# A selective scan with steps spread over GpSimd and ScalarE, and a softmax filter run as a three-tile pipeline

## The chip, the cores and the metric

The kernel is one program on one core of a Trainium2 chip. The metric is device time in microseconds (us) from launch to end; lower is better. The median of three runs of the kernel before is 19240.01 us (19239.32 to 19246.41).

## What is computed

The input is a float32 image batch of 4 x 64 channels x 64 x 64. Four layers follow one another; the change touches parts of three of them.

- Layer 0: convolutions, normalisation, and then a selective scan (Mamba) over all 4 x 4096 tokens with 128 inner channels and 16 states. Each image starts from a state of zero.
- Layer 1: two selective scans over rows and over columns, with 192 inner channels and 96 states. Nothing of it is changed.
- Layer 2: a filter. A 3x3 convolution to 32 channels, a leaky ReLU and a 1x1 convolution give nine logits for each pixel; their softmax gives nine weights.
- Layer 3: a second selective scan of 16 states over one sequence of 16384 tokens, then projection, layer norm, SiLU and a residual.

The core of the two scans and of the filter:

```python
def step(h, t):                       # 16 states, 128 channels
    d, b, c, xt = t                   # d: softplus step, xt: silu of a 4-tap convolution
    h = h * jnp.exp(d[:, None] * A) + (d * xt)[:, None] * b[None, :]
    return (h, h @ c)
y = (ys + xc * D) * jax.nn.silu(z)    # out projection (and in layer 3: layer norm, silu, + x)

w_lp = softmax(conv1x1(leaky(conv3x3(x))))         # layer 2: nine weights a pixel
w_hp = delta_center - w_lp
high = sum over the 9 shifts k of shifted(x, k) * w_hp[k]
return x + high
```

## The kernel before, in words

A sequence of stages shares the core; each is a block with its own instruction streams, joined by semaphores, and streams are hand-ordered. In time: `phase_conv_norm` (to 274 us), `phase_mamba` for layer 0 (to 1616 us; here **m0**), two `phase_axis` stages (to 17242 us), `phase_filter` (to 17757 us), `phase_mamba` for layer 3 (to the end; here **m3**, the one with `final`). The names in the profile have lost their stage digits: `m_` is both m0 and m3.

**The scan stages.** Tokens go in 32 tiles of 512. For each tile `i` and state `n` of 16, the engines do this:

- TensorE (PE): `pb` (L662) spreads B's row n over 128 partitions into one of three PSUM banks, `pc` (L664) spreads C's row n, and `add` (L650) sums an earlier `gv` into `py`. `pb` waits until the scan three states back has freed its bank.
- ScalarE (ACT): `av` (L570) is exp(dt * A), `cv` (L573) copies `pc` out of PSUM. `pc` n waits for `cv` n-1.
- VectorE (DVE): the product `pb * dx` (L462), and one state behind it the scan (L468), which writes `hs`.
- GpSimd (POOL): `gv = hs * cv` (L604). Nothing else.

Between these, at a fixed state n, each engine has steps of the tile ahead (i+1) and the tile behind (i-1). For the tile ahead PE runs `in_proj` (L625; two matmuls, waits for the tile's input `u`), `gate_proj`, `x_proj`, `dt_proj`. ACT runs two tanh, `high`, `softplus`, then `middle` (L539), a logarithm (L543) and, in m3, the logarithm and exponential of `rsqrt` (L552, L554). DVE runs `silu` (L410, L412), `gates`, `remainder` (L420), `low` and `steps` (dt L428, dx L430). For the tile behind DVE runs `gated`, and in m0 `out_plain`, in m3 `norm` and `out_silu` (L453, L457). Two matmul forms occur throughout: bf16 ones, and float32 ones, which the trace shows as two records each.

After state 15 DVE copies the last column of all 16 states to `st` times `keep` (L501), and waits for it; every scan of the next tile starts from `st`. A product of tile i+1 also waits for dx.

SyncE (SP) issues all DMAs in one order: for each i it waits for `gate_proj` of i, loads `u` for i+2 (L338, L339), waits until the output tile `ot` of i is done (`s_done`), stores it (L345) and loads the residual for i+2 (L342). So the input for tile i+3 is issued only after output i is done:

```python
sync.wait_ge(s_xz, i + 1)
load_input(i + 2, p)
sync.wait_ge(s_done, i + 1)
store(i)
load_residual(i + 2, p)
```

In m3 the output of i is done by `out_silu(i)`, the last thing that DVE does in tile i+1; PE's `in_proj(i+3)` stands at n = 4 of tile i+2.

**The filter stage.** 16 tiles of two half-batches, one after another, in one chain: nine 3x3 taps (L1602, float32 matmuls), bias on ACT, leaky ReLU on DVE (L1543), logits, softmax in small DVE steps (L1545 to L1557) with one Exp on ACT, transpose by PE (L1618), copy on ACT, then for each of nine weights a float32 matmul with `sel` (L1626, two PSUM banks) that spreads it over the channels, a DVE product with the shifted image (L1566) and a DVE add (L1574), last `2 x - total` (L1577), and six stores. The taps of tile i+1 stand between the logits and the transpose of tile i.

Of the kernel before, what the change touches and what calls it, by code (L numbers as in the profile page):

```python
# [12 lines left out]
F32 = mybir.dt.float32  # L13
# [8 lines left out]
TOK = 512  # L22
# [202 lines left out]
def phase_mamba(nc, sem, ident_in, tag, w, u_s, res_s, out_s, reset, final):  # L225
# [6 lines left out]
    with ExitStack() as ctx:  # L232
# [79 lines left out]
        s_sq, s_var, s_rs, s_pn, s_tn = (sem(tag + n) for n in ("squares", "var", "rstd", "normed", "silu_tanh"))  # L312
# [10 lines left out]
        with nc.Block() as block:  # L323
# [40 lines left out]
            def _(dve):  # L364
# [12 lines left out]
                if reset:  # L377
                    v.memset(keep[:].rearrange("p (b t) -> p b t", t=TPB)[:, :, TPB - 1], 0.0)
# [47 lines left out]
                def steps(T, tp):  # L426
                    dve.wait_ge(s_sp, T + 1)
                    v.tensor_tensor(dt[:, tp], dt[:, tp], sp[:], ALU.add).then_inc(s_dt, 1)  # L428
                    dve.wait_ge(s_dt, T + 1)
                    v.tensor_tensor(dx[:, tp], dt[:, tp], xc[:], ALU.mult).then_inc(s_dx, 1)  # L430

# [4 lines left out]
                def residual_ready(T, tp):  # L436
                    dve.wait_ge(s_res[tp], T * 8 + (16 if tp == 0 else 8))

                def out_plain(T, tp):
                    dve.wait_ge(s_o, T + 1)  # L440
                    dve.wait_ge(s_out, 16 * T + 16)
                    residual_ready(T, tp)
                    v.tensor_tensor(ot[:], py[0:C, tp], res[:, tp], ALU.add).then_inc(s_done, 1)

                def norm(T):
                    dve.wait_ge(s_rs, T + 1)
                    v.tensor_tensor(n3[:], n1[:], n2[:], ALU.mult).then_inc(s_pn, 1)
                    dve.wait_ge(s_pn, 3 * T + 1)
                    v.tensor_scalar(n1[:], n3[:], half[:, 1:2], half[:, 2:3], ALU.mult, ALU.add).then_inc(s_pn, 1)

                def out_silu(T, tp):
                    dve.wait_ge(s_tn, T + 1)
                    v.scalar_tensor_tensor(n3[:], n2[:], 1.0, n1[:], ALU.add, ALU.mult).then_inc(s_pn, 1)  # L453
                    dve.wait_ge(s_pn, 3 * T + 3)
                    dve.wait_ge(s_out, 16 * T + 16)
                    residual_ready(T, tp)
                    v.tensor_tensor(ot[:], n3[:], res[:, tp], ALU.add).then_inc(s_done, 1)  # L457
# [6 lines left out]
                def scan(i, n):  # L464
                    un = i * NS + n
# [1274 lines left out]
```

## Time and profile before

| what | us |
|---|---|
| median of three runs | 19240.01 |
| the profiled execution | 19243.72 |
| span of its instructions | 19241.8 |
| m0, filter, m3 (by window) | 1342, 515, 1485 |
| busy: PE, DVE, ACT, POOL | 16257.4, 17802.0, 13962.1, 15292.2 |

Busy time is a mean over stages with other limits; the two axis stages take 15626 us of the span. A timeline row gives the start, the duration and, in brackets, the idle time of that engine before it and what ended it; the duration of a DVE instruction is longer than the distance to the next one's start, as they overlap by about 0.1 us. A matmul row with x2 is one float32 matmul.

### The profile page before, as it was taken

What the parts mean: (1) busy time and instruction counts of PE and PEld (TensorE: products, weight loads), DVE (VectorE), ACT (ScalarE), POOL (GpSimd) and SP (SyncE); (2) the same over time, 40 slices, a digit from 0 to 9 for tenths busy, and PEclk for the clock granted to TensorE, in tenths of its full rate; (3) what the DMA queues carried; (4) which work ended last, traced back from release to release, by engine and by line L of the source; (5) the groups of instructions that cost most, each with busy time, mean ns of one, the idle gap of its engine ahead of it and who ended that gap; (6) DMA issues with size and microseconds to landing.
All of it is one profiled execution on the core that took longest, in us unless ns stands there. A gap on an engine that the chain in (4) does not pass through costs nothing. (4 is left out here: it accounts for less than half of the span.)

```text
span 19241.8 us, 290646 instructions
## 1 busy us (share of the span) xinstructions
PE 16257.4 (84%) x60328; PEld 8303.8 (43%) x60424; DVE 17802.0 (93%) x48666; ACT 13962.1 (73%) x18390; POOL 15292.2 (79%) x10500
## 2 busy tenths in 40 slices
PE   5776888888888888888688888888888888887777
PEld 2223444444444444444344444444444444442222
DVE  4998999999999999999899999999999999984888
ACT  4665777777777777777577777777777777761666
POOL 1554999889888998888699999999999999970444
PEclk8998999999999999999899999999999999996999
DMA  1000000000000000000000000000000000000000
GB/s 33 13 13 12 11 11 11 11 11 11 11 11 11 11 11 11 11 11 11 12 11 11 11 11 11 11 11 11 11 11 11 11 11 11 11 10 20 10 12 11
DMA packets 778173, 227.53 MB, mean 12 GB/s; under 512 B 747760, under 2 KB 750476, under 8 KB 776332
## 3 DMA queue, kind: packets, MB, share of 16 engines
q1 hardware_dynamic: 776332, 206.79, 8.2%
q8 instruction: 691, 11.32, 0.3%
q14 instruction: 1150, 9.42, 0.2%
HBM read 143.66 MB, written 62.97 MB: 11 GB/s over the span
## 5 line engine op out<-in xcount | busy, mean ns | idle before, releaser
L1222 POOL TENSOR_TENSOR h_sm<-h_sm,h_wr 128x768 f32<-128x768 f32 x2944 | 5400.3, 1834 | 755.2 <-DVE h_wr L1002 669.6
L1222 POOL TENSOR_TENSOR w_sm<-w_sm,w_wr 128x768 f32<-128x768 f32 x2944 | 5399.1, 1834 | 502.5 <-DVE w_wr L1002 404.6
L1386 PE MATMUL w_pz<-w_xr,w_tri 128*128 128x384 f32 x9984 | 4462.6, 530 | 788.2 <-DVE w_wr L1002 622.5
L1386 PE MATMUL h_pz<-h_xr,h_tri 128*128 128x384 f32 x9984 | 4424.7, 526 | 770.6 <-DVE h_wr L1002 604.5
L1002 DVE SCALAR_TENSOR_TENSOR h_wr<-h_pz,h_bct,h_rbuf 128x192 f32<-128x192 f32 x11776 | 4250.3, 407 | 171.9 <-PE h_pz L1386 171.2
L1002 DVE SCALAR_TENSOR_TENSOR w_wr<-w_pz,w_bct,w_rbuf 128x192 f32<-128x192 f32 x11776 | 4243.4, 408 | 96.1 <-PE w_pz L1386 95.5
L976 DVE SCALAR_TENSOR_TENSOR w_xr<-w_cbuf,w_bct,w_pdx 128x192 f32<-128x192 f32 x9984 | 3634.9, 405 | 76.0 <-issue 35.2
L976 DVE SCALAR_TENSOR_TENSOR h_xr<-h_cbuf,h_bct,h_pdx 128x192 f32<-128x192 f32 x9984 | 3632.6, 404 | 75.7 <-issue 35.2
L1098 ACT ACTIVATE h_cbuf<-h_pe_e,h_consts 128x1024 f32<-128x1024 f32 x2304 | 2526.1, 1112 | 1532.4 <-PE h_pe_e L1374 1332.1
L1098 ACT ACTIVATE w_cbuf<-w_pe_e,w_consts 128x1024 f32<-128x1024 f32 x2304 | 2526.1, 1112 | 1492.7 <-PE w_pe_e L1374 1305.1
L604 POOL TENSOR_TENSOR m_gv<-m_hs,m_cv 128x512 f32<-128x512 f32 x1024 | 1351.0, 1322 | 2240.9 <-DVE m_hs L468 2213.4
L1121 ACT ACTIVATE w_rbuf<-w_pe_e,w_consts 128x1024 f32<-128x1024 f32 x2304 | 2476.3, 1113 | 0.0
L1121 ACT ACTIVATE h_rbuf<-h_pe_e,h_consts 128x1024 f32<-128x1024 f32 x2304 | 2476.2, 1113 | 0.0
L1386 PEld LDWEIGHTS w_pz<-w_xr,w_tri 128*128 128x128 f32 x9984 | 1516.5, 191 | 2027.4 <-DVE w_wr L1002 1647.7
L1386 PEld LDWEIGHTS h_pz<-h_xr,h_tri 128*128 128x128 f32 x9984 | 1516.5, 191 | 1974.5 <-DVE h_wr L1002 1604.6
L1374 PE MATMUL h_pe_e<-h_decay,h_lt 128*128 128x256 bf16 x9216 | 1782.1, 275 | 105.3 <-ACT h_rbuf L1121 88.8
L1374 PE MATMUL w_pe_e<-w_decay,w_lt 128*128 128x256 bf16 x9216 | 1773.2, 274 | 105.6 <-ACT w_rbuf L1121 88.7
L1374 PEld LDWEIGHTS h_pe_e<-h_decay,h_lt 128*128 128x128 bf16 x9216 | 915.3, 101 | 1337.2 <-issue 679.2
L1374 PEld LDWEIGHTS w_pe_e<-w_decay,w_lt 128*128 128x128 bf16 x9216 | 895.6, 99 | 1277.9 <-issue 709.0
L468 DVE TENSOR_TENSOR_SCAN m_hs<-m_av,m_st,m_pb 128x512 f32<-128x512 f32 x1024 | 1292.5, 1267 | 55.7 <-ACT m_av L570 54.7
L1231 POOL TENSOR_TENSOR w_cbuf<-w_cbuf,w_dxs 128x384 f32<-128x384 f32 x1152 | 1155.2, 1003 | 90.6 <-issue 67.6
L1231 POOL TENSOR_TENSOR h_cbuf<-h_cbuf,h_dxs 128x384 f32<-128x384 f32 x1152 | 1155.8, 1003 | 22.8 <-DVE h_dxs L986 22.8
(355 smaller groups left out, 19595.9 us busy)
## 6 DMA issues: line engine op xcount, KB each, us to landing
h_lt<-pieces_s SPq DMA_DIRECT2D x512, 96.0 KB, 4.4
w_lt<-pieces_s SPq DMA_DIRECT2D x512, 96.0 KB, 4.3
pieces_s<-h_pieces SPq DMA_DIRECT2D x384, 48.0 KB, 2.1
pieces_s<-w_pieces SPq DMA_DIRECT2D x384, 48.0 KB, 2.1
h_xt<-first_s SPq DMA_DIRECT2D x34, 128.0 KB, 5.5
w_xt<-first_s SPq DMA_DIRECT2D x34, 128.0 KB, 3.1
m_u<-hn_s SPq DMA_DIRECT2D x32, 128.8 KB, 2.7
m_u<-slots_s SPq DMA_DIRECT2D x32, 128.8 KB, 2.6
```

What stands on the lines that cost most here:

```text
L468: v.tensor_tensor_scan(hs[:, n, :], av[:, n % UB, :], pb[:, BANK[n], :], st[:, n:n + 1], ALU.mult, ALU.add).then_inc(s_h, 1)
L604: g.tensor_tensor(gv[:, n % GV, :], hs[:, n, :], cv[:, n % UB, :], ALU.mult).then_inc(s_g, 1)
L976: ins = v.scalar_tensor_tensor(xr[:, P % 3, m * DX:(m + 1) * DX], cbuf[:, ch % 2, (n + m) % 16, :], bct[:, par, g * 2 * NX + n + m:g * 2 * ...
L1002: ins = v.scalar_tensor_tensor(dst, pz[:, P % 2, m * DX:(m + 1) * DX], bct[:, par, g * 2 * NX + NX + n + m:g * 2 * NX + NX + n + m + 1], r ...
L1098: a.activation(cbuf[:, ch % 2, :, 64 * j:64 * j + 64].rearrange("p n (b d) -> p b n d", b=2), pe_e[:, G % 2 * 2:G % 2 * 2 + 2, :].rearrang ...
L1121: a.activation(rbuf[:, ch % 2, :, 64 * j:64 * j + 64].rearrange("p n (b d) -> p b n d", b=2), pe_e[:, G % 2 * 2:G % 2 * 2 + 2, :].rearrang ...
L1222: tt(sm[:, g], sm[:, g], wr[:, u % 3], ALU.add).then_inc(s_add, 1)
L1231: tt(c2, c2, dxs[:, g:g + 1, :].broadcast_to([128, 2, DX]), ALU.mult).then_inc(s_xo, 1)
L1374: mm = t.matmul(dst, lt[:, par, g * JQ + m, :], decay[:, m, n0:n0 + 16, :], start=True, stop=True)
L1386: t.matmul(pz[:, P % 2, 0:2 * DX], tri[:], x, start=True, stop=True).then_inc(s_z, 1)
```

## The change

In the scan stages the two SiLU operations on DVE read PSUM and one SBUF tile each, instead of one PSUM tile and then two SBUF tiles. `steps` (dt, dx) moves to POOL, behind gv of n = 13. The state's copy moves from DVE to ACT in m0 (`keep_state`, before scan 0 of the next tile) and is gone in m3, where a scan starts from the last column of `hs`. In m3 the norm product moves to POOL behind gv of n = 12, scale and shift to ACT, and the last sum (`out_final`, which signals `s_done`) to POOL behind gv of n = 15. PE's `in_proj` moves from n = 4 to n = 1 and 2, `gate_proj` from 5 to 3, `x_proj` from 9 to 7, `dt_proj` from 10 to 9; the ACT and DVE steps of the tile ahead move one state earlier. SyncE's order in the scan stages is untouched.

In the filter, taps of tile T+2, logits and softmax of T+1 and products of T stand in one iteration. The weights are split in three bf16 parts (96 rows), so that `sel` is a bf16 matmul in three banks; the weights are negated and 2 is added to the centre one, in place of the last `2 x - total`; nine products go to nine buffers and their eight sums to POOL; `ot` has two buffers.

```diff
                 def silu(T):
-                    v.tensor_scalar(v0[:], pf[:], cbh[:, 0:1], None, ALU.add).then_inc(s_v, 1)
+                    v.scalar_tensor_tensor(v0[:], pf[:], cbh[:, 0:1], th[:], ALU.add, ALU.mult).then_inc(s_v, 1)
                     dve.wait_ge(s_v, T + 1)
-                    v.scalar_tensor_tensor(xc[:], th[:], 1.0, v0[:], ALU.add, ALU.mult).then_inc(s_xc, 1)
+                    v.scalar_tensor_tensor(xc[:], pf[:], cbh[:, 0:1], v0[:], ALU.add, ALU.add).then_inc(s_xc, 1)
...
-                def scan(i, n):
+                def scan(i, n, first):
                     un = i * NS + n
+                    if n == 0 and not first:
+                        if reset:
+                            dve.wait_ge(s_st, i)
+                        else:
+                            dve.wait_ge(s_h, i * NS + UB)
+                    kept = st[:, n:n + 1] if first or reset else hs[:, n, TOK - 1:TOK]
                     dve.wait_ge(s_b, un + 3)
                     dve.wait_ge(s_a, un + 1)
-                    v.tensor_tensor_scan(hs[:, n, :], av[:, n % UB, :], pb[:, BANK[n], :], st[:, n:n + 1],
+                    v.tensor_tensor_scan(hs[:, n, :], av[:, n % UB, :], pb[:, BANK[n], :], kept,
                                          ALU.mult, ALU.add).then_inc(s_h, 1)
...
-                            scan(i, n - 1)
+                            scan(i, n - 1, not before)
+                        if behind and n == 5:
+                            silu(i + 1)
+                        if behind and n == 6:
+                            gates(i + 1, 1 - p)
-                        if behind and n == 6:
-                            silu(i + 1)
...
-                        if behind and n == 11:
+                        if behind and n == 10:
...
-                        if behind and n == 13:
+                        if behind and n == 12:
...
-                        if behind and n == 14:
-                            steps(i + 1, 1 - p)
-                        if before and n == 13 and final:
-                            norm(i - 1)
-                    scan(i, NS - 1)
-                    dve.wait_ge(s_h, i * NS + NS + UB)
-
-                    v.tensor_scalar(st[:], hs[:, :, TOK - 1], keep[:, bass.ds(i, 1)], None, ALU.mult).then_inc(s_st, 1)
-                    dve.wait_ge(s_st, i + 1)
-                    if before and final:
-                        out_silu(i - 1, 1 - p)
+                        if before and n == 14 and final:
+                            out_silu(i - 1, 1 - p)
+                    scan(i, NS - 1, not before)
...
+                def tanh_out(T, tp):
+                    act.wait_ge(s_pn, T + 1)
+                    a.activation(py[0:C, tp], n3[:], ACT.Identity, bias=half[:, 2:3], scale=half[:, 1:2])
+                    a.activation(n2[:], n3[:], ACT.Tanh, bias=half[:, 2:3], scale=half[:, 1:2]).then_inc(s_tn, 1)
+
+                def keep_state(i):
+                    act.wait_ge(s_h, i * NS + UB)
+                    a.activation(st[:], hs[:, :, TOK - 1], ACT.Identity, scale=keep[:, bass.ds(i, 1)]).then_inc(s_st, 1)
...
                         a.activation(av[:, n % UB, :], dt[:, p], ACT.Exp, scale=amat[:, n:n + 1]).then_inc(s_a, 1)
+                        if n == 0 and before and reset:
+                            keep_state(i)
...
                         a.activation(cv[:, n % UB, :], pc[:], ACT.Copy).then_inc(s_c, 1)
+                        if behind and n == 3:
+                            tanhs(i + 1)
...
+                        if behind and n == 8:
+                            high(i + 1, 1 - p)
                         if behind and n == 9:
-                            high(i + 1, 1 - p)
-                        if behind and n == 10:
                             softplus(i + 1, 1 - p)
-                        if behind and n == 12:
+                        if behind and n == 11:
                             middle(i + 1, 1 - p)
...
-                        if before and n == 12 and final:
+                        if before and n == 11 and final:
                             rsqrt(i - 1, 1 - p)
-                        if before and n == 14 and final:
-                            tanh_out(i - 1)
+                        if before and n == 13 and final:
+                            tanh_out(i - 1, 1 - p)
...
+                def steps(T, tp):
+                    pool.wait_ge(s_sp, T + 1)
+                    tt(dt[:, tp], dt[:, tp], sp[:], ALU.add).then_inc(s_dt, 1)
+                    pool.wait_ge(s_dt, T + 1)
+                    pool.wait_ge(s_xc, T + 1)
+                    tt(dx[:, tp], dt[:, tp], xc[:], ALU.mult).then_inc(s_dx, 1)
...
+                def norm(T):
+                    pool.wait_ge(s_rs, T + 1)
+                    if not (isinstance(T, int) and T == 0):
+                        pool.wait_ge(s_done, T)
+                    tt(n3[:], n1[:], n2[:], ALU.mult).then_inc(s_pn, 1)
...
+                def out_final(T, tp):
+                    pool.wait_ge(s_ns, T + 1)
+                    pool.wait_ge(s_out, 16 * T + 16)
+                    pool.wait_ge(s_res[tp], T * 8 + (16 if tp == 0 else 8))
+                    tt(ot[:], n3[:], res[:, tp], ALU.add).then_inc(s_done, 1)
...
-                        g.tensor_tensor(gv[:, n % GV, :], hs[:, n, :], cv[:, n % UB, :], ALU.mult).then_inc(s_g, 1)
+                        tt(gv[:, n % GV, :], hs[:, n, :], cv[:, n % UB, :], ALU.mult).then_inc(s_g, 1)
+                        if before and n == 12 and final:
+                            norm(i - 1)
+                        if behind and n == 13:
+                            steps(i + 1, 1 - p)
+                        if before and n == 15 and final:
+                            out_final(i - 1, 1 - p)
...
+                def in_proj(T, tp, m, first):
+
+                    if m == 0:
+                        pe.wait_ge(s_u[tp], T * 16 + (32 if tp == 0 else 16))
+                        if not first:
+                            pe.wait_ge(s_rest, T)
+                    t.matmul(pf[:], tapw[:, m, :], u[:, tp, 2 * m:2 * m + TOK], start=(m == 0), stop=(m == 1))
...
-                        if behind and n == 4:
-                            in_proj(i + 1, 1 - p, False)
-                        if behind and n == 5:
+                        if behind and n in (1, 2):
+                            in_proj(i + 1, 1 - p, n - 1, False)
+                        if behind and n == 3:
                             gate_proj(i + 1, 1 - p, False)
...
+                        if behind and n == 7:
+                            x_proj(i + 1)
...
                         if behind and n == 9:
-                            x_proj(i + 1)
-                        if behind and n == 10:
                             dt_proj(i + 1)
...
-        sel = sb("sel", [2 * K9, K9, 2, C])
+        sel = sb("sel", [3 * REP, K9, 2, C], BF16)
...
-        pr = sb("pr", [128, 2, TOK])
...
-        pw = ps("pw", [128, 2, TOK])
...
+        pw = ps("pw", [128, 3, TOK])
...
+                        sp.wait_ge(s_sum, i * (K9 - 1) + 2 * (K9 - 1))
...
+                def product(T, n):
+                    dve.wait_ge(s_wb, T * K9 + n + 1)
+                    dve.wait_ge(s_sum, T * (K9 - 1) + max(n, 1))
+                    v.tensor_tensor(pr[:, n, :].rearrange("p (r c) -> p r c", c=W),
+                                    pw[:, n % 3, :].rearrange("p (r c) -> p r c", c=W),
+                                    acc[:, bass.ds(row(T) + n // 3, ROWS), n % 3:n % 3 + W], ALU.mult).then_inc(s_pr, 1)
...
+                for T, p, half, more, behind in tiles(dve):
+                    for n in range(K9):
+                        product(T, n)
+                        if more and n == 1:
+                            shifted(T + 1)
+                        if more and n == 3:
+                            softmax(T + 1)
+                            spread(T + 1)
+                        if more and n == 7:
+                            remainder(T + 1, 1 - p)
+                    if behind:
+                        leaky(T + 2)
+                    if more:
+                        low(T + 1, 1 - p)
...
+                for T, p, half, more, behind in tiles(act):
+                    if more:
+                        exps(T + 1)
+                        high(T + 1, 1 - p, None if isinstance(T, int) and T == 0 else T * K9)
+                    if behind:
+                        biased(T + 2)
+                    if more:
+                        middle(T + 1, 1 - p)
...
+                for T, p, half, more, behind in tiles(pool):
+                    for n in range(1, K9):
+                        pool.wait_ge(s_pr, T * K9 + n + 1)
+                        pool.wait_ge(s_sum, T * (K9 - 1) + K9 - 1 + n - 1)
+                        if n == K9 - 1:
+                            pool.wait_ge(s_out[p], half * 16 * OUTS + 16 * OUTS)
+                        tt(ot[:, p, :] if n == K9 - 1 else total[:], pr[:, 0, :] if n == 1 else total[:], pr[:, n, :],
+                           ALU.add).then_inc(s_sum, 1)
...
+                def turned(T):
+                    pe.wait_ge(s_nw, T * 2 + 2)
+                    if not (isinstance(T, int) and T == 0):
+                        pe.wait_ge(s_rest, T)
...
+                def spread(T, p, n):
+                    if n == 0:
+                        pe.wait_ge(s_wt, T + 1)
+                    if n >= 3 or not (isinstance(T, int) and T == 0):
+                        pe.wait_ge(s_pr, T * K9 + n - 2)
+                    t.matmul(pw[:, n % 3, :], sel[:, n].rearrange("p g c -> p (g c)"), wt[:, p, :], start=True,
+                             stop=True).then_inc(s_wb, 1)
...
+                TAPS = ((0,), (1,), (2, 3), (4, 5), (6,), (7,), (8,), (), ())
+                for T, p, half, more, behind in tiles(pe):
+                        spread(T, p, n)
+                        if more and n == 0:
+                            logits(T + 1)
+                        if more and n == 5:
+                            turned(T + 1)
+                        if behind:
+                            for k in TAPS[n]:
+                                conv(T + 2, k)
```

## Rows read from the trace of the kernel before

**Rows 1.** Busy time by stage: window, length, then each engine, PE clock, DMA
```profile
274.00:1616.00 1342.00, 1006.75 (x2450) 374.13 (x2498) 1204.41 (x1372) 834.02 (x1345) 675.21 (x512) 0.91 0.05 13
...
17242.00:17757.00 515.00, 424.26 (x832) 159.17 (x832) 223.15 (x410) 45.04 (x64) 0.00 (x0) 0.66 0.08 17
17757.00:19242.00 1485.00, 1046.35 (x2520) 391.94 (x2568) 1275.39 (x1472) 924.31 (x1509) 675.75 (x512) 0.90 0.04 12
```

**Rows 2.** The state's copy in m0 and m3: ns min/median/max, first and last start
```profile
L501 DVE TENSOR_SCALAR m_st<-m_hs,m_keep x32: 235/1285/1297, 354.2 to 1605.1; 128x16 f32<-128x16 f32 x32
...
L501 DVE TENSOR_SCALAR m_st<-m_hs,m_keep x32: 234/1283/1292, 17834.3 to 19225.3; 128x16 f32<-128x16 f32 x32
```

**Rows 3.** DVE's timeline in one tile of m0: start, duration, operation
```profile
614.11 1.22 DVE L412 SCALAR_TENSOR_TENSOR m_xc<-m_th,m_v 128x512 f32<-128x512 f32 x1
...
622.20 1.26 DVE L468 TENSOR_TENSOR_SCAN m_hs<-m_av,m_st,m_pb 128x512 f32<-128x512 f32 x1
623.38 0.66 DVE L462 TENSOR_TENSOR m_pb<-m_pb,m_dx 128x512 f32<-128x512 f32 x1
...
633.80 0.67 DVE L428 TENSOR_TENSOR m_dt<-m_dt,m_softplus 128x512 f32<-128x512 f32 x1
634.50 1.64 DVE L430 TENSOR_TENSOR m_dx<-m_dt,m_xc 128x512 f32<-128x512 f32 x1
636.07 0.68 DVE L462 TENSOR_TENSOR m_pb<-m_pb,m_dx 128x512 f32<-128x512 f32 x1
...
639.24 1.28 DVE L501 TENSOR_SCALAR m_st<-m_hs,m_keep 128x16 f32<-128x16 f32 x1
640.66 1.30 DVE L462 TENSOR_TENSOR m_pb<-m_pb,m_dx 128x512 f32<-128x512 f32 x2
```

**Rows 4.** POOL's product in m3: ns min/median/max
```profile
L604 POOL TENSOR_TENSOR m_gv<-m_hs,m_cv x512: 1262/1271/1762, 17797.4 to 19225.4; 128x512 f32<-128x512 f32 x171
```

**Rows 5.** PE's timeline in m0, behind the table loads
```profile
632.76 0.39 PE L664 MATMUL m_pc<-m_bc,m_sel 128*128 128x512 bf16 x1 [2.95 <-ACT m_cv L573]
...
634.25 0.63 PE L662 MATMUL m_pb<-m_bc,m_sel 128*128 128x512 bf16 x1
```

**Rows 6.** DVE's and ACT's timelines in one tile of m3
```profile
18408.32 0.67 DVE L420 TENSOR_TENSOR m_rest<-m_pf,m_bc 128x512 f32<-128x512 f32 x1
...
18415.15 0.70 ACT L570 ACTIVATE m_av<-m_dt,m_amat 128x512 f32<-128x512 f32 x1
```

**Rows 7.** Output and next input in m3: DVE's and SP's timelines, DMA landing
```profile
18425.92 0.68 DVE L457 TENSOR_TENSOR m_ot<-m_n,m_res 64x512 f32<-64x512 f32 x1 [0.23 <-DVE m_n L453]
...
18428.78 0.47 SPq L339 DMA_DIRECT2D m_u<-slots_s  x1
...
m_u<-slots_s SPq DMA_DIRECT2D x1, 128.5 KB, 2.6
```

**Rows 8.** PE's timeline in m3: behind a long wait, and at full clock
```profile
18416.39 0.39 PE L664 MATMUL m_pc<-m_bc,m_sel 128*128 128x512 bf16 x1 [4.40 <-ACT m_cv L573]
18416.62 1.67 PE L650 MATMUL m_py<-m_gv,m_ident 128*128 128x512 f32 x2
...
18431.42 0.38 PE L664 MATMUL m_pc<-m_bc,m_sel 128*128 128x512 bf16 x1
18431.63 1.02 PE L650 MATMUL m_py<-m_gv,m_ident 128*128 128x512 f32 x2
18432.49 1.88 PE L625 MATMUL m_pf<-m_u,m_tapw 128*128 128x512 f32 x4
```

**Rows 9.** DVE's timeline in the filter, one tile to the next
```profile
17476.52 0.68 DVE L1543 SCALAR_TENSOR_TENSOR f_h<-f_h 64x512 f32<-64x512 f32 x1
...
17493.00 0.69 DVE L1566 TENSOR_TENSOR f_total<-f_pw,acc 128x512 f32<-128x512 f32 x1 [11.99 <-PE f_pw L1626]
...
17507.93 0.68 DVE L1543 SCALAR_TENSOR_TENSOR f_h<-f_h 64x512 f32<-64x512 f32 x1 [0.21 <-issue]
```

**Rows 10.** DVE's timeline in the filter's preparation
```profile
17249.84 1.34 DVE L1532 COPY f_sel<-f_ident 18x1152 f32<-18x1152 f32 x1
```

More of the change, by code:

```diff
@@ L617, in _ @@
                 pe.wait_ge(s_ready, 1)
-                def in_proj(T, tp, first):
-                    pe.wait_ge(s_u[tp], T * 16 + (32 if tp == 0 else 16))
-                    if not first:
-                        pe.wait_ge(s_rest, T)
-                    for m in range(2):
-                        t.matmul(pf[:], tapw[:, m, :], u[:, tp, 2 * m:2 * m + TOK], start=(m == 0), stop=(m == 1))
+                def in_proj(T, tp, m, first):
[4 more added lines that the diff above has]
+                    t.matmul(pf[:], tapw[:, m, :], u[:, tp, 2 * m:2 * m + TOK], start=(m == 0), stop=(m == 1))
                 def gate_proj(T, tp, first):
@@ new lines, in _ @@
+                leaky(0)
+                shifted(0)
+                softmax(0)
+                spread(0)
+                leaky(1)
+                remainder(0, 0)
+                low(0, 0)
+                for T, p, half, more, behind in tiles(dve):
[12 more added lines that the diff above has]
+                        low(T + 1, 1 - p)
@@ L1590, in _, with high, middle @@
                     a.activation(ex[:], lg[:], ACT.Exp).then_inc(s_ex, 1)
-                    act.wait_ge(s_t, i + 1)
-                    a.activation(wt[:], pt[0:2 * K9, :], ACT.Copy).then_inc(s_wt, 1)
+                def high(T, p, used):
+                    act.wait_ge(s_t, T + 1)
+                    if used is not None:
+                        act.wait_ge(s_wb, used)
+                    a.activation(wt[:, p, :], pt[0:3 * REP, :], ACT.Copy).then_inc(s_hi, 1)
+                def middle(T, p):
+                    act.wait_ge(s_rest, T + 1)
+                    a.activation(wt[0:2 * REP, p, :], rest[0:2 * REP], ACT.Copy).then_inc(s_mid, 1)
@@ L1596, in _, with conv, logits @@
                 t = nc.tensor
-                def conv(i, r):
-                    if not isinstance(i, int) or i > 0:
-                        pe.wait_ge(s_h1, i)
-                    for n in range(K9):
-                        mm = t.matmul(ph[0:2 * MID, :], w1[:, n].rearrange("p g m -> p (g m)"),
-                                      acc[:, bass.ds(r + n // 3, ROWS), n % 3:n % 3 + W],
-                                      start=(n == 0), stop=(n == K9 - 1))
-                    mm.then_inc(s_h, 1)
-                def weights(i, next_row):
-                    pe.wait_ge(s_h2, i + 1)
+                pe.wait_ge(s_go, 1)
+                def conv(T, n):
+                    if n == 0 and not (isinstance(T, int) and T == 0):
+                        pe.wait_ge(s_h1, T)
+                    mm = t.matmul(ph[0:2 * MID, :], w1[:, n].rearrange("p g m -> p (g m)"),
+                                  acc[:, bass.ds(row(T) + n // 3, ROWS), n % 3:n % 3 + W],
+                                  start=(n == 0), stop=(n == K9 - 1))
+                    if n == K9 - 1:
+                        mm.then_inc(s_h, 1)
+                def logits(T):
+                    pe.wait_ge(s_h2, T + 1)
+                    if not (isinstance(T, int) and T == 0):
+                        pe.wait_ge(s_lx, T)
                     for m in range(BLK):
```

245 lines of the change are left out of this document (125 added, 120 removed).

## The prediction

> **What bounds the kernel now.** I read the busy time by stage first, then the distance from tile to tile, then DVE's timeline of one tile, and last what each idle stretch waited for. The change touches 3342 of 19242 us: m0 1342, the filter 515, m3 1485 [rows 1]. In m0 DVE is busy 1204 of 1342 us, so DVE sets the pace. In m3 it is busy 1275 of 1485; the rest is waits. In the filter no engine is full for long: DVE has 223 of 515, and PE's 424 are at a mean clock of 0.66. That stage is a chain, with one wait of 12.0 us in each tile of 31.4 [rows 9].
>
> A tile takes (1605.1 - 354.2) / 31 = 40.35 us in m0 and (19225.3 - 17834.3) / 31 = 44.87 us in m3 [rows 2].
>
> **m0.** One state costs DVE 0.60 for the product and 1.18 for the scan by starts [rows 3], so 16 cost 28.5. Seven operations that stay (gated, two of SiLU, gates, out_plain, remainder, low) cost 0.6 to 0.7 each, 4.4 in all: 32.9. What goes: dt and dx 2.27 (633.80 to 636.07), the state's copy with its wait 1.42 (639.24 to 640.66), and 0.56 as the second SiLU operation falls from 1.22 to the 0.66 of one that reads PSUM and a single SBUF tile [rows 3]. That is 4.25. The remaining 40.35 - 32.9 - 4.25 = 3.2 are waits.
>
> The state's copy costs nothing on ACT: it takes about 0.25 us there (DVE's shortest is 0.235, [rows 2]), while DVE does products 0 and 1 (1.2 us). If ACT were over 0.9 us late, scan 0 would wait. New waits:
> - PE at states 1 to 3 gets two `in_proj`, the `diag` matmul and `gate_proj`. A bf16 matmul takes 0.21, a float32 one 0.86 [rows 8], so a state costs PE 0.21 + 0.21 + 0.86 = 1.3 and those four 3.4. Walked from product 0, with three banks of lead, `pb` 3 comes 0.35 and `pb` 4 1.25 late: 1.6. The old tanh wait, most of the 3.2, goes for it.
> - Behind ACT's table loads PE restarts at half clock after 2.95 idle: from 632.76 to the end of `pb`, 634.88, where DVE's product could start at 633.8 [rows 5]. dt and dx covered that. Now it costs 1.1, and 0.5 at the next state.
> - dx on POOL: gv of n = 13 starts 1.5 after scan 13 starts; gv, dt and dx take 1.27 each [rows 4] with small gaps: ready at 5.5. DVE reaches product 0 at 1.19 + 0.60 + 1.19 + 1.19 = 4.2, plus the 0.5 above: 0.9 of waiting.
>
> Sum 32.9 + 4.1 = 37.0, so 31 x 3.35 = **-104**. With none of the new waits it is -231, with all doubled +23; I keep the walk, as each term has its row, and put 60 on either side.
>
> DVE's dx takes 1.64 where dt takes 0.67 [rows 3], and the state's copy 1.28 where its shortest takes 0.235 [rows 2]: beside a running POOL product of 1.27 an operation with two SBUF tiles waits. The Trainium skill (GPSIMD Engine Reference, Engine selection) speaks against the move: elementwise work belongs on VectorE, as GpSimd is about twice slower with two inputs. Row and rule agree on 1.27 against 0.67; by the rule alone dt and dx cost 1.2 more in a tile and m0 gives 31 x 1.2 = 37 less.
>
> **m3.** The same 32.9 (out_silu in place of out_plain), then three waits. Remainder to the end of `av` took 7.5 us [rows 6]; ACT will come to `middle` about 0.8 earlier, as softplus stands further ahead, so 6.7, and DVE is at its scan after 5.4: 1.3. norm waits on POOL for gv 12, then two ACT operations: out_silu can start 12.1 after remainder where DVE is there at 9.7: 2.4. PE's front costs 1.6 as in m0. With 0.8 for smaller ones this gives 39.
>
> But SP's order stays. The input for tile i+3 is issued after `s_done` of i, which is now POOL's `out_final`, behind gv of n = 15 in tile i+1, and `in_proj(i+3)` now stands at n = 1 of tile i+2. Before, the last sum ended at 25.92 + 0.68 = 26.60, the second load was issued at 28.78 and landed 2.6 later, at 31.4 [rows 7]; `in_proj` ran at 32.5 [rows 8], 1.1 us of slack. This closes a ring:
> - From the end of out_final, E: the input lands at 4.9. PE has idled some 8 us. After 4.40 idle a float32 matmul took 1.67 in place of 1.02 [rows 8], so `in_proj` and `pb` 2 end at 7.3. DVE then does nine states (16.0), gated, silu and gates (2.5), and waits 2.8 for `pb` 3 and 4: remainder at E + 28.6.
> - From remainder: scan 12 at 6.7, gv 12 to 9.5, norm to 10.8, gv 13 behind `pb` 14 and scan 13 11.9 to 13.2, dt, dx, gv 14, gv 15, out_final, each 1.3 on POOL: 19.8.
>
> The ring is 48.4. At full clock behind the wait it is 45.6. I take 48: 29 x 3.1 = +91, two tiles without it -12: **+79**. Bounds: 39 per tile (-182) and 50 (+137).
>
> The Trainium skill (TensorE: Matmul & The Clock Gate, HAM oscillation) says that a wait for data in every tile makes each tile begin at half clock. Rows 8 agree; by the rule the ring is 48.4, without it 45.6, and m3 would be 81 us apart between the two.
>
> **The filter.** Three tiles overlap. One iteration on PE at full clock: nine taps of 0.86 and nine bf16 matmuls of 0.22 [rows 8], logits and transpose about 1 each: 11.7. PE stops for the last product, leaky and `low` on DVE before the next tile's first matmul, so it starts at half clock: +2 (three float32 matmuls at 0.65 more each, [rows 8]). It waits about 1.1 for the softmax on DVE, five small operations between products. The tail is 0.6 + 0.6 + 0.7, half a POOL sum for each of the two with two SBUF tiles (1.3), and semaphores 0.3: 3.5. Sum 18.3; I take 18.5. POOL's eight sums, 8 x 1.3 = 10.4, hide in that. The whole: before the first product 39 (loads 9, three copies of 1.34 [rows 10] and clearing 5, taps twice 18, softmax, transpose and split 7), 14 x 18.5 = 259, then 14 and 12 for the last tiles, 2 for stores: 326 against 515: **-189**. Bounds: 14.5 per tile without half clock and lock waits (-245), 26.5 with PE at half clock throughout (-72).
>
> **Sum.** The profiled execution, 19243.7, - 104 - 189 + 79 = 19029.7; the median lies 3.7 below that execution, too little to move it: **19030**. 0.2% (38 us) is what a measurement can tell.
>
> **Rivals.**
> - The input load stays hidden in m3: 39 per tile, -182: 19243.7 - 104 - 189 - 182 = 18769. For it: it was hidden before. Against it: 1.1 us of slack, and `in_proj` comes three states (some 5 us) earlier while the last sum comes later on a POOL queue full of gv and dx. 14%.
> - The filter's PE stays at half clock, as it does in long stretches now (mean 0.66, [rows 1]): 19243.7 - 104 - 72 + 79 = 19147. Against it: a PE that falls behind has no gaps, and a mean of 0.66 means that it reaches full clock in part of each tile already. 8%.
> - Slower: the ring in m3 holds PE at half clock for the whole tile. PE's work, 16 x 1.3 + 8 x 0.86 = 27.7, becomes 55.4, with 5 of waiting 60: 29 x 15.1 - 12 = +427, 19378. It makes the kernel slower from a ring of 44.87 + (293 + 12) / 29 = 55.4 on. Against it: after 4.40 idle full clock was back within 15 us [rows 8]. 4%.
> - The change does not do what it says on DVE: SiLU with one SBUF tile still waits for POOL. Then 63 x 0.56 = 35 come back: 19065. Against it: `pb * dx`, PSUM and one SBUF tile, takes 0.66 beside POOL [rows 3]. 2%.
>
> **Numbers.** My forecast has 72%. It spans ±60 in m0, +0 to +137 in m3, -245 to -100 in the filter, which together is some ±120. The range 18755 to 19165 holds nine tenths of it (0.65), the second and fourth rivals (0.10) and the upper half of the first (0.07); the third lies outside. Faster 0.92, same 0.03, slower 0.05.
>
> **What would show it.** In m0: L501's work on ACT, tiles 37 apart, DVE waiting for dx by 1 us at each product 0. In m3: PE's first `in_proj` waiting for the DMA of `u` in 29 tiles, 5 to 8 us each, and DVE's product 2 behind it; tiles 48 apart, window 1565. If that wait is absent and tiles are 39 apart, the first rival holds. In the filter: tiles 18.5 apart, POOL busy 8 x 1.27 in each, clock above 0.8. A filter stage over 400 us, or m0 tiles over 40, would make the forecast wrong from another side.

## The result, and the profile after

| | before | after |
|---|---|---|
| median, four runs each, side by side (us) | 19241.79 | 19107.51 (19091.68 to 19113.85) |
| span of the profiled execution | 19241.8 | 19112.1 |
| mean granted clock of PE | 0.961 | 0.964 |

The ratio is 0.9927, 95% interval 0.9913 to 0.9941: 134 us faster, where 210 were forecast. The page of the kernel after, busy time by engine:

```profile
PE 16120.1 (84%) x60280; PEld 8249.4 (43%) x60280; DVE 17478.0 (91%) x48304; ACT 13984.3 (73%) x18454; POOL 15672.6 (82%) x10820
```

DVE gave up 324 us of work and the kernel only 134, so more than half of what was freed turned into waiting. Where, the busy time by stage tells (m0, axis, filter, m3; columns as in [rows 1]):

```profile
275.50:1534.80 1259.30, 980.15 (x2498) 370.12 (x2498) 1087.72 (x1276) 841.33 (x1376) 743.42 (x576) 0.94 0.05 14
1534.80:17171.00 15636.20, 13653.64 (x54300) 7336.53 (x54300) 15068.84 (x45347) 12071.40 (x15372) 13943.60 (x9472) 0.98 0.09 11
17171.00:17529.30 358.30, 256.89 (x688) 89.61 (x688) 201.71 (x336) 35.98 (x65) 165.46 (x128) 0.80 0.11 24
17529.30:19112.00 1582.70, 1087.20 (x2568) 401.69 (x2568) 1087.81 (x1280) 948.38 (x1541) 819.92 (x640) 0.88 0.04 11
```

In m3 DVE has 188 us less to do than before (1275.39 in [rows 1]) and the stage is some 98 longer. The filter lost 157 us and m0 some 82. For the comparisons below I cut each run at DVE's clearing instruction at the head of each stage, and took the tile from DVE's gated product, first to last start by 31:

| us | m0 | axis | filter | m3 | m0 tile | m3 tile |
|---|---|---|---|---|---|---|
| before | 1336.0 | 15626.3 | 515.6 | 1483.7 | 40.19 | 44.69 |
| after | 1253.8 | 15636.3 | 358.2 | 1582.8 | 37.55 | 47.84 |
| e1_load_first | 1251.1 | 15625.8 | 360.8 | 1317.9 | 37.48 | 39.30 |
| e2_late_in_proj | 1269.7 | 15620.7 | 361.3 | 1472.1 | 38.01 | 44.21 |
| e3_before_load_first | 1330.8 | 15633.2 | 515.7 | 1490.8 | 40.09 | 44.94 |
| e4_steps_on_dve | 1283.0 | 15625.5 | 361.4 | 1369.2 | 38.55 | 40.96 |
| e5_filter_warm | 1251.3 | 15626.0 | 327.1 | 1582.8 | 37.47 | 47.84 |
| e6_leaky_last | 1252.1 | 15620.6 | 357.0 | 1326.1 | 37.51 | 39.53 |
| e7_front_spread | 1235.0 | 15619.3 | 359.2 | 1304.4 | 37.04 | 38.92 |
| e8_both | 1235.7 | 15635.5 | 356.8 | 1303.1 | 37.04 | 38.86 |
| e9_front_and_warm | 1236.9 | 15642.9 | 325.3 | 1307.2 | 37.06 | 39.02 |
| e10_warm_leaky_last | 1235.9 | 15628.0 | 321.1 | 1306.5 | 37.04 | 39.00 |

The axis stages, which nothing touches, differ by up to 24 us between profiled executions. So a few us of the total tell nothing here, and stage lengths do.

**m3: who waits for the input.** The instructions of the kernel after that write or read `m_u`, in m3; the answer ends with who waited for its DMA (sum in us, times):

```profile
  DMA m_u<-slots_s: 412.1, 58
...
  PEld m_pf L640: 218.0, 29
  PE m_pf L640: 194.0, 29
```

29 tiles, 6.7 us each, on PE's matmuls (194.0 / 29). One of them in the timeline (POOL, SP, PE and DVE rows in order of time; columns as in [rows 3]):

```profile
18427.44 1.25 POOL L601 TENSOR_TENSOR m_ot<-m_n,m_res 64x512 f32<-64x512 f32 x1
...
18430.87 0.47 SPq L340 DMA_DIRECT2D m_u<-slots_s  x1
...
18433.58 2.08 PE L640 MATMUL m_pf<-m_u,m_tapw 128*128 128x512 f32 x2 [6.42 <-DMA m_u<-slots_s]
...
18435.44 0.63 PE L678 MATMUL m_pb<-m_bc,m_sel 128*128 128x512 bf16 x1
18436.12 0.70 DVE L444 TENSOR_TENSOR m_pb<-m_pb,m_dx 128x512 f32<-128x512 f32 x1 [8.11 <-PE m_pb L678]
...
18457.69 0.66 DVE L421 TENSOR_TENSOR m_rest<-m_pf,m_bc 128x512 f32<-128x512 f32 x1
...
18464.88 1.28 DVE L456 TENSOR_TENSOR_SCAN m_hs<-m_av,m_hs,m_pb 128x512 f32<-128x512 f32 x1 [1.52 <-ACT m_av L553]
...
18476.24 1.26 POOL L601 TENSOR_TENSOR m_ot<-m_n,m_res 64x512 f32<-64x512 f32 x1
```

out_final ends at 18428.69, the second load is issued 2.2 later and PE has it at 4.9. `in_proj` takes 2.08, `pb` 0.63 (0.39 elsewhere), both at half clock behind 6.42 of idle. DVE has stood still for 8.11 us when it does product 2. The next out_final starts 48.8 after this one.

**The filter.** PE and DVE at the turn of a tile of the kernel after:

```profile
17387.65 0.68 DVE L1621 TENSOR_TENSOR f_rest<-f_pt,f_wt 96x512 f32<-96x512 f32 x1
17388.25 0.68 DVE L1631 TENSOR_TENSOR f_pr<-f_pw,acc 128x512 f32<-128x512 f32 x1
17388.85 0.90 DVE L1588 SCALAR_TENSOR_TENSOR f_h<-f_h 64x512 f32<-64x512 f32 x1
17389.78 1.63 DVE L1625 TENSOR_TENSOR f_wt<-f_rest,f_wt 32x512 bf16<-32x512 f32 x1
...
17391.55 0.60 PE L1747 MATMUL f_pw<-f_wt,f_sel 96*128 96x512 bf16 x1 [4.53 <-DVE f_wt L1625]
17392.08 1.89 PE L1729 MATMUL f_pl<-f_w,f_h 64*128 64x18 f32 x8
17393.91 1.97 PE L1718 MATMUL f_ph<-acc,f_w 128*64 x2
...
17397.69 1.09 DVE L1597 TENSOR_TENSOR f_lg<-f_lg,f_mx 128x72 f32<-128x72 f32 x1
```

PE stops for 4.53 us and comes back at half clock: 1.89 for the logits, 1.97 for a tap. The last line is one of the small softmax operations. Its neighbours of that size read at most one SBUF tile and take 0.22; it reads two and takes 1.0 to 1.1 in 15 tiles, beside POOL's sums, and 0.23 in the first, where POOL has no sum yet.

### The profile page after: what moved, and what is told of

The parts are those of the page before. It is cut to its first block and busy times, and to the rows that moved or that the text cites. A ratio compares the mean times of both kernels' runs of the same rounds, so it can differ in the third digit from the quotient of the medians.

```text
span 19112.1 us, 290534 instructions
## 1 busy us (share of the span) xinstructions
PE 16120.1 (84%) x60280; PEld 8249.4 (43%) x60280; DVE 17478.0 (91%) x48304; ACT 13984.3 (73%) x18454; POOL 15672.6 (82%) x10820
## 5 line engine op out<-in xcount | busy, mean ns | idle before, releaser
L992 DVE SCALAR_TENSOR_TENSOR h_xr<-h_cbuf,h_bct,h_pdx 128x192 f32<-128x192 f32 x9984 | 3635.8, 405 | 73.5 <-issue 32.9
L444 DVE TENSOR_TENSOR m_pb<-m_pb,m_dx 128x512 f32<-128x512 f32 x1024 | 699.1, 688 | 527.4 <-PE m_pb L678 511.1
```

The source lines that it names most:

```text
L444: v.tensor_tensor(pb[:, BANK[n], :], pb[:, BANK[n], :], dx[:, p], ALU.mult).then_inc(s_b, 1)
L992: ins = v.scalar_tensor_tensor(xr[:, P % 3, m * DX:(m + 1) * DX], cbuf[:, ch % 2, (n + m) % 16, :], bct[:, par, g * 2 * NX + n + m:g * 2 * ...
```

## The experiments

**e1_load_first.** The kernel after, with SP's load of `u` ahead of its wait for the output; a load still waits for the `in_proj` and `gate_proj` that free its buffer:

```diff
+                sync.wait_ge(s_xz, 1)
+                load_input(2, 0)
...
-                        sync.wait_ge(s_xz, i + 1)
-                        load_input(i + 2, p)
+                        sync.wait_ge(s_xz, i + 2)
+                        load_input(i + 3, 1 - p)
                         sync.wait_ge(s_done, i + 1)
                         store(i)
                         load_residual(i + 2, p)
...
```

> The changed kernel, but SyncE issues the input of tile i+3 before it waits for the output of tile i (both scan stages). Ring theory: the 29 waits of PE for the DMA of u in m3 are gone, DVE's product 2 loses its wait of 8 us, m3's tiles fall from 47.8 to about 39 us: 29 x 8.8 = 256 less, total 18850 (18800 to 18900); m0 stays at 37.5. Rival, POOL's backlog behind dt, dx and out_final sets m3: tiles stay above 45, total above 19050. Rival, another wait takes over half of it: tiles 42 to 44.

Measured: 18848.63 us, ratio to before 0.9796 [0.9779, 0.9812], m3 tile 39.30. No matmul or weight load waits for `u` any more; of those who wait for what `u` gives, one line is left (m3):

```profile
  ACT m_th L508: 83.6, 32
```

The ring is the whole excess of m3: 259 us of the kernel after (265 in the stage m3) went with the order of two steps in SP's queue. POOL has the same work in both kernels (15672.6 and 15663.1 us busy), so its backlog behind dt, dx and out_final, the rival, did not set the tile. 39 was the forecast's tile without a ring.

**e2_late_in_proj.** The kernel after, with the front where it was before, SP's order kept:

```diff
-                        if behind and n in (1, 2):
-                            in_proj(i + 1, 1 - p, n - 1, False)
-                        if behind and n == 3:
+                        if behind and n == 4:
+                            in_proj(i + 1, 1 - p, 0, False)
+                            in_proj(i + 1, 1 - p, 1, False)
+                        if behind and n == 5:
                             gate_proj(i + 1, 1 - p, False)
```

(tanh, SiLU and gates go one or two states later, too.)

> The changed kernel with SyncE's order as it is, but in_proj back at n = 4, gate_proj at 5, tanh at 4, silu at 6, gates at 7. Ring theory: the load lands before n = 4, so PE's DMA waits shrink to under 1 us each and m3's tiles fall to 40 to 42 us, while the old tanh wait adds about 1 us a tile in m0 (38.5). Total 18950 (18900 to 19010). Rival, the place of in_proj does not matter: m3's tiles stay at 47 to 48, total near 19130.

Measured: 19004.28 us in one run, m3 tile 44.21, and in m3:

```profile
  PE m_pf L640: 65.4, 29
```

The wait falls from 6.7 to 2.3 us a tile but stays in all 29. It was expected under 1 us, and the tile at 40 to 42, so this is a miss: the ring is only shortened, by 3.6 us, though `in_proj` moved by two or three states. In the kernel before, with `in_proj` at the same n = 4, PE waited for `u` 3 times, 0.7 us in all; here, with the later output and less work in a tile, the ring stays closed from n = 4, and the earlier `in_proj` tightens it. Of what was tried, only the order in SP's queue opens it. m0 loses 16 us with the front in its old place, the tanh, SiLU and gates steps moved with it.

**e3_before_load_first.** The edit of e1 on the kernel before.

> The kernel before with SyncE's order as in e1_load_first. Ring theory: there was 1.1 us of slack and PE waited for u 3 times, 0.7 us in all, so nothing changes: 19240, ratio 1.000, m3's tiles 44.9. Rival, the late load already cost time before: tiles below 44.

Measured: 19248.52 us, ratio 1.000 [0.999, 1.001], m3 tile 44.94 (44.69). The order of the queue cost nothing before; the new schedule made it cost.

**e4_steps_on_dve.** On e1, dt and dx go back from POOL to DVE at n = 13 (the added lines are DVE's, the lines taken out POOL's):

```diff
+                steps(0, 0)
...
+                        if behind and n == 13:
+                            steps(i + 1, 1 - p)
...
-                steps(0, 0)
...
-                        if behind and n == 13:
-                            steps(i + 1, 1 - p)
```

> e1_load_first with dt and dx back on DVE, behind scan 12 of n = 13. By my walk DVE does 2.27 us more a tile, gets back the wait for dx (0.3 in m0) and about 1 us of waits for pb behind the table loads: +1.0 a tile in m0 and 0 to +1 in m3, 30 to 60 us slower than e1_load_first. Rival, POOL is the wrong place for them: e4 is 30 us faster than e1.

Measured: 18920.07 us, ratio 0.9833 [0.9816, 0.9849], 71 more than e1, where 30 to 60 was expected: 1.07 a tile in m0, as expected (1.0), and 1.66 in m3, more than expected (0 to 1). By stage that is 32 and 51, together 83; the two profiled executions lie 84 apart and the medians 71. DVE's dx, in m0:

```profile
L440 DVE TENSOR_TENSOR m_dx<-m_dt,m_xc x31: 691/1636/1644, 310.9 to 1474.8; 128x512 f32<-128x512 f32 x31
```

1.64 beside POOL; its shortest, 0.69, is that of the first tile, while POOL has nothing to do yet. On POOL it takes 1.27. The Trainium skill (GPSIMD Engine Reference, Engine selection) would put both on VectorE. Here that costs 71 us, as DVE does the most in both stages and its dx is held up by POOL anyway.

**e5_filter_warm.** The kernel after, with twenty matmuls into a spare PSUM bank that nobody reads, behind each filter tile; what is computed is the same:

```diff
+        idle = ps("idle", [128, TOK])
...
+                    if more:
+                        for k in range(20):
+                            t.matmul(idle[:], sel[:, 0].rearrange("p g c -> p (g c)"), wt[:, p, :], start=True, stop=True)
```

> The changed kernel with 20 bf16 matmuls into a spare PSUM bank at the end of each filter tile, where PE otherwise waits 4.5 us for the last weights; their result is not used. Clock theory: logits (1.9 us) and the first two taps (2.0 and 1.4) run at half clock only because of that wait; at full clock they give back 0.9 + 1.1 + 0.5, so the filter's tiles fall from 20.5 to 18.0 us and the stage from 358 to about 325. Rival, the chain on DVE and POOL sets the tile and the clock does not matter: 20.5 stays. Total 19075 in the first case, 19107 in the second.

Measured: 19068.47 us in one run, filter stage 327.1. PE's timeline there:

```profile
17389.65 4.48 PE L1770 MATMUL f_idle<-f_wt,f_sel 96*128 96x512 bf16 x20
17394.35 0.39 PE L1748 MATMUL f_pw<-f_wt,f_sel 96*128 96x512 bf16 x1 [0.22 <-DVE f_wt L1626]
17394.67 1.06 PE L1730 MATMUL f_pl<-f_w,f_h 64*128 64x18 f32 x8
17395.66 1.07 PE L1719 MATMUL f_ph<-acc,f_w 128*64 x2
17396.66 0.39 PE L1748 MATMUL f_pw<-f_wt,f_sel 96*128 96x512 bf16 x1
17396.98 1.07 PE L1719 MATMUL f_ph<-acc,f_w 128*64 x2
```

The stall is as long, but filled, and what follows runs at full clock: 1.06 for 1.89, 1.07 for 1.97. A tile takes 18.0 in place of 20.5 and the stage 31 us less; the forecast had +2 a tile for it, measured are 2.5. The Trainium skill (TensorE: Matmul & The Clock Gate, HAM oscillation) says that a DMA wait that is long enough makes each tile start at half clock. The filter agrees, though its wait is one for DVE: 1.89 and 1.97 behind the stall of 4.53. Behind m0's wait of 2.95 only some of the tiles do.

**e6_leaky_last.** On e1, another order on DVE at the end of a filter tile:

```diff
-                    if behind:
-                        leaky(T + 2)
                     if more:
                         low(T + 1, 1 - p)
+                    if behind:
+                        leaky(T + 2)
```

> e1_load_first with leaky behind low in the filter. Tail theory: the next tile's first matmul waits for low, and low waits for leaky and for a running sum on POOL; low starts 0.8 us earlier and falls between two sums, so a tile gives back about 1.5 us, the stage 21 us (338). Rival, POOL's sums set the tile: stage stays at 360.

Measured: 18836.08 us in one run, filter stage 357.0, 4 less than e1 and not the 21 expected: a miss. PE in that filter:

```profile
17369.23 0.39 PE L1756 MATMUL f_pw<-f_wt,f_sel 96*128 96x512 bf16 x1 [2.85 <-DVE f_wt L1634]
17370.82 1.46 PE L1738 MATMUL f_pl<-f_w,f_h 64*128 64x18 f32 x6 [1.20 <-DVE f_h L1597]
```

(The timeline's window ends within the logits.) The first spread waits 2.85 in place of 4.53, but the logits then wait 1.20 for `leaky`. Most of the wait is moved, not gone. e6 leaves open whether the half clock behind it held the tile at 20.5, or that wait.

**e7_front_spread.** On e1, `in_proj` one state earlier, and the `diag` matmul at n = 2, apart from `gate_proj` at n = 3:

```diff
-                        if behind and n in (1, 2):
-                            in_proj(i + 1, 1 - p, n - 1, False)
+                        if behind and n in (0, 1):
+                            in_proj(i + 1, 1 - p, n, False)
...
-                        if n == LAG - 1:
+                        if n == 2:
                             t.matmul(py[:, p], diag_d[:], ...
```

> e1_load_first with PE's four front matmuls one state each: in_proj at n = 0 and 1, diag at 2, gate_proj at 3. Front theory: DVE's wait for pb at n = 4 (1.43 us) comes from three float32 matmuls at n = 3; it falls to about 0.6, the others stay: 0.8 to 1.2 less in each of 62 tiles, 50 to 75 us less than e1 (18775 to 18800). Rival, the PE work only has to be done and the wait moves to n = 1 to 3: within 15 us of e1.

Measured: 18806.68 us, ratio 0.9774 [0.9757, 0.979], 42 less than e1, where 50 to 75 was expected. By stage m0 gives 16 and m3 13, 0.4 in each tile and not 0.8 to 1.2: half a miss. The other 12 are no more than stages vary by. `pb` 4 in m0, in e1 and then in e7, at the same place of a tile:

```profile
661.15 0.70 DVE L453 TENSOR_TENSOR m_pb<-m_pb,m_dx 128x512 f32<-128x512 f32 x1 [1.43 <-PE m_pb L687]
```
```profile
654.30 0.70 DVE L453 TENSOR_TENSOR m_pb<-m_pb,m_dx 128x512 f32<-128x512 f32 x1 [0.57 <-PE m_pb L687]
```

0.86 less, which is one float32 matmul: the wait fell as expected (to 0.6). That the other waits stay, as was expected, failed. In m0 the product behind ACT's table loads, n = 14, waits 1.43 on the mean of 29 tiles, for 1.03 in e1:

```profile
675.79 0.61 PE L689 MATMUL m_pc<-m_bc,m_sel 128*128 128x512 bf16 x1 [2.95 <-ACT m_cv L567]
676.19 1.91 PE L674 MATMUL m_py<-m_gv,m_ident 128*128 128x512 f32 x2
```

PE comes back from this wait of 2.95 at half clock in 25 of 30 tiles, in e1 in 10 of 30, with 12 more in between. In m3 it is products 1 and 2 that wait 0.4 longer together.

**e8_both.** On e7 the order of e6, `middle` ahead of the bias on ACT, and two taps moved to the end of the tile:

```diff
-                TAPS = ((0,), (1,), (2, 3), (4, 5), (6,), (7,), (8,), (), ())
+                TAPS = ((0,), (1,), (2, 3), (4,), (5,), (6,), (), (), (7, 8))
```

> e7_front_spread with leaky behind low, and in the filter the last two taps behind the last weights, so that PE works on them while DVE does the tail; middle ahead of the bias on ACT. Tail theory: 1.5 us from low, 1.7 from two taps and about 1 from the clock, tiles of 16.5 instead of 20.5, stage near 305, total 55 us under e7. Rival, POOL or the half clock holds the tile at 19 or more: under 25 us less than e7.

Measured: 18809.02 us, ratio 0.9772 [0.9756, 0.9788]; filter stage 356.8, where about 305 was expected, and 2 us above e7 where 55 less was expected. A clear miss. PE there, from one first spread on:

```profile
17349.71 0.39 PE L1756 MATMUL f_pw<-f_wt,f_sel 96*128 96x512 bf16 x1 [2.10 <-DVE f_wt L1634]
17351.29 1.46 PE L1738 MATMUL f_pl<-f_w,f_h 64*128 64x18 f32 x8 [1.20 <-DVE f_h L1597]
17352.68 1.97 PE L1727 MATMUL f_ph<-acc,f_w 128*64 x2
...
17355.12 1.97 PE L1727 MATMUL f_ph<-acc,f_w 128*64 x2
...
17357.56 2.44 PE L1727 MATMUL f_ph<-acc,f_w 128*64 x4
```

The tile stays at 20.5. The stall is shorter, but PE waits twice in it, and it runs at half clock into the third group of taps (1.97, 1.97, and 2.44 for two that take 1.93 at full clock). By these rows, that and the second wait give back what the moved taps free; how much falls to the clock is not shown, as no run has the moved taps together with the spare matmuls of e5.

**e9_front_and_warm** and **e10_warm_leaky_last.** e7 with the spare matmuls of e5, and the same with e6's order.

> The spread front matmuls one product earlier, the input load put ahead of the store, and twenty spare matmuls behind each filter tile. If the filter's half clock and the front's place are independent of each other, this takes what the spare matmuls took by themselves (filter stage 358.2 to 327.1, 31 us) off the 18806.7 of the version without them: 18775 us, filter stage 326 to 328 us, m3 tile 38.9, m0 tile 37.0. If the earlier front matmuls had bought their 42 us by something that the filter shares, it stays above 18790.

> As the version beside it, with the low split ahead of the leaky step on VectorE in the filter. Moving the low split earlier by itself gave only 4 us, and the tile stayed at 20.5. If that was because PE, at half its clock after the stall, sets the tile's length, then with the clock kept up the order must count: the low split ends 0.8 to 1.6 us earlier in each of some 14 tiles, 11 to 22 us, so 18760 us and a filter stage of 305 to 316 us. Rival: it was because the logits then wait for the leaky step (1.2 us) instead of for the split, at either clock; then nothing changes and it comes out within 5 us of the version beside it, filter stage 324 to 330 us.

Measured: e9 18792.19 us, ratio 0.9757 [0.974, 0.9773], filter stage 325.3. Its total is 17 above the forecast and just over the 18790 that was set as the sign against it. By stage it is otherwise: the filter stage is 34 shorter than in e7, the tiles of m0 and m3 are within 0.1 of e7's, and the untouched axis stages are 24 longer. So the two gains do add. e10: 18775.04 us, ratio 0.9748 [0.9732, 0.9764], filter stage 321.1. The total is 17 less than e9, but the untouched axis stages are 15 of it. The filter stage is 4 less, which lies outside both forecasts (305 to 316, and 324 to 330 for the rival) and nearer to the rival's. A tile falls from 18.0 to 17.6, where 0.8 to 1.6 was expected of the clock; at half clock the same order changes it by under 0.1, and e6 has its 4 us in the first few tiles. So at full clock the order counts for 0.4 a tile. DVE and PE in e10:

```profile
17374.05 0.73 DVE L1635 TENSOR_TENSOR f_wt<-f_rest,f_wt 32x512 bf16<-32x512 f32 x1
17374.81 1.64 DVE L1598 SCALAR_TENSOR_TENSOR f_h<-f_h 64x512 f32<-64x512 f32 x1
```
```profile
17371.89 4.48 PE L1779 MATMUL f_idle<-f_wt,f_sel 96*128 96x512 bf16 x20
17376.20 0.38 PE L1757 MATMUL f_pw<-f_wt,f_sel 96*128 96x512 bf16 x1
17376.51 1.06 PE L1739 MATMUL f_pl<-f_w,f_h 64*128 64x18 f32 x8
```

The second of the two DVE operations ends at 17376.45 and the logits, which need `leaky`, start at 17376.51. `low` took 1.63 as the second and takes 0.73 as the first, `leaky` 0.90 and 1.64: whoever comes second meets POOL's last sum. The spare matmuls end at 17376.2, so the first spread could have come 1.4 earlier with fewer of them; that was not tried, and the logits could not have followed it, as they need `leaky`. The ratios of e9 and e10 lie within each other's intervals; either is some 2.5% faster than the kernel before, against 0.7% for the change.

## Why the prediction was right or wrong

The time fell, and the range held it; it came out 77 us above the forecast. By stage, profiled spans:

| | forecast | measured |
|---|---|---|
| m0 | -104 | -82 |
| filter | -189 | -157 |
| m3 | +79 | +99 |
| axis, not touched | 0 | +10 |

**m3, the mechanism: right.** The ring exists, at the place and with the wait that were forecast: 29 tiles, 6.7 us each on PE (5 to 8). Each link from the end of out_final, E, in the rows above: input at E + 4.9 (4.9), product 2 at E + 7.4 (7.3), remainder at E + 29.0 (28.6); from there scan 12 at 7.2 (6.7) and the end of out_final at 19.8 (19.8). The ring is 48.8 and not 48.4. e1 took it away and nothing else: 39.30 for the 39 of the first rival. That rival fell by the trace of after, and e3 shows that the queue's order alone is harmless. The tile of e1 holds 33.8 of work and 5.9 of waits on the mean of 29, for the forecast's 32.9 and 6.1. The ring at full clock, 45.6, stays an estimate: no run fills that stall.

**m3, the size: 20 short.** The mis-sized term is "I take 48", in "29 x 3.1 = +91, two tiles without it -12". Its own sum was 48.4, and 29 tiles took 48.9 on the mean: 0.9 a tile, 25 us. Against that, the tile before was set at 44.87, a mean over all 31 intervals, of which the last is much shorter; the same 29 took 45.3, which takes 12 off. So the ring costs 29 x 3.6 = 104. The other two tiles gave back 6 and not 12, and 2 lie outside the tiles.

**m0: 22 short.** The waits were right in sum, and the base was not. Over the first 29 intervals a tile took 38.0, where the forecast had 37.0: 33.8 of work with its small gaps, for 32.9, and 4.2 of waits, for 4.1. In the parts, on the mean of 29 tiles:

| waits of DVE in an m0 tile, us | forecast | measured |
|---|---|---|
| the front (products 2, 3, 4) | 1.6 | 0.45 + 0.27 + 1.43 = 2.2 |
| behind the table loads (13, 14, 15) | 1.1 + 0.5 | 0.03 + 1.07 + 0.59 = 1.7 |
| product 0 | 0.9 | 0.4 |

The base took sixteen states at 1.78 and seven operations at their best spacing; the tile has gaps of about 0.1 in several places, and the first SiLU operation takes 0.76 by starts. The term for dx was too high: DVE comes later than I walked it, and in the m0 stage only 18 products wait for dx, 9.5 us in all. The longer tile after is 29 us of the error; the tile before was 40.7 and not 40.35, which takes 10 off; the last two intervals add 2. Copy, dt and dx left DVE, the copy takes ACT 0.32, and each SiLU operation on DVE takes 0.73 to 0.75, so the fourth rival is out.

PE's half clock behind the table loads [rows 5] comes in some tiles and not in others, after the same 2.95 us of idle. Two tiles of the kernel after, PE's rows and DVE's product behind them:

```profile
687.34 0.39 PE L680 MATMUL m_pc<-m_bc,m_sel 128*128 128x512 bf16 x1 [2.95 <-ACT m_cv L558]
687.57 1.02 PE L665 MATMUL m_py<-m_gv,m_ident 128*128 128x512 f32 x2
688.85 0.70 DVE L444 TENSOR_TENSOR m_pb<-m_pb,m_dx 128x512 f32<-128x512 f32 x1 [0.37 <-PE m_pb L678]
...
761.76 0.61 PE L680 MATMUL m_pc<-m_bc,m_sel 128*128 128x512 bf16 x1 [2.95 <-ACT m_cv L558]
762.16 1.92 PE L665 MATMUL m_py<-m_gv,m_ident 128*128 128x512 f32 x2
764.54 0.70 DVE L444 TENSOR_TENSOR m_pb<-m_pb,m_dx 128x512 f32<-128x512 f32 x1 [1.65 <-PE m_pb L678]
```

Of 30 such waits in m0, 7 end at full clock (1.02 to 1.04 for the float32 matmul), 11 at half clock (1.91) and 12 in between; DVE then waits 0.37 to 1.65, and tiles are 37.2 to 38.7 long. The forecast took one tile's row for all, and its 1.1 comes close to the mean.

**The filter: 32 short.** Its tile is 20.4 on the mean of 14 and not 18.5 (18.3 by the sum): 27 of the 32. Another 7 lie behind the last of these tiles (35 us for 28), and the stretch before the first product was 2 shorter. Two steps of the tile fell. The tail of 3.5 is 4.53: I let DVE do leaky and `low` right behind the last product, but the last spread and product come behind the remainder, and `low` has to wait for POOL's sum for 0.9 (1.63, and 0.73 where it is free of it, in e10). And "nine taps of 0.86 and nine bf16 matmuls of 0.22" held for matmuls of one kind in a row: with a spread between single taps the starts in e5 are 1.00 and 0.32 apart, so that PE's full-clock part is 18.0 - 4.5 = 13.5 in place of 11.7. The 1.1 of waiting for the softmax did not show in e5. The +2 for half clock was near: 2.5. Together 13.5 + 2.5 + 4.5 = 20.5. The second rival is out, as the stage's clock is 0.80 and its tile 20.5, not 26.5; its price in the forecast is off by 5, too, as 14 x 8 = 112 leaves 77 and not 72. POOL, with 165 of 358 us, is not the limit.

**Sum.** The profiled execution came out 84 above the forecast: 22 + 32 + 20 = 74 by the three stages, and about 10 in stages that the change does not touch, which is within what they vary by. The median lies 6 below that execution, which leaves the 77. All three errors of the tiles after have one sign: a walk from row to row gives the least that a tile can take, and I took it as what it would take. That the total still fell within the range is owed to its width of some 120 us on either side.

**The rule against the move to POOL** that the prediction cites from the Trainium skill (GPSIMD Engine Reference, Engine selection) would have m0 37 us worse than I forecast. m0 was 22 worse, but not by that rule: in e4, without the move, m0 is slower by 32 and the kernel by 71.

## What to carry to other kernels

When steps move between engines, follow each buffer round to its next load: the last operation of a tile may release a DMA that is queued behind it, and an earlier reader of that DMA closes a ring that no busy share shows. Put loads ahead of waits for outputs on an in-order queue, even where it brings nothing yet. Then look at the engine that stalls once in every tile, and ask what its clock does behind the stall.

## What the runs showed of the hardware

- Twenty matmuls that nobody reads are worth 31 us in a stage of 358 (e5; 34 in e9): they take 4.48 us of a stall of 4.5 and the next tile starts at full clock, 2.4 GHz and not 1.2.
- The same 2.95 us of idle at the same place in a tile was followed by half clock in some tiles and by full clock in others, within one execution: 11 and 7 of 30 in m0 of the kernel after, 25 and 5 of 30 in e7. What decides between them stays open.
- A DVE operation with two SBUF tiles can be held up by nearly the whole of the POOL product beside it, small ones too: 1.09 for 128x72 where its neighbours take 0.22, 1.64 for 128x512 where its shortest took 0.69.
